# Layer 1's output stage and routing in one: tokens routed image by image, output bias added in layer 0, normalisation on ScalarE, experts read out first

## The reference, cut to what matters

```python
# x: (4, 56, 56, 256): B = 4 images of N = 3136 tokens, C = 256, float32
x = x + L0_conv_ref(gn(x), ...)            # layer 0: 7x7 neighbourhood attention, ends in out @ Wp + bp
t = to_tokens(x)
t = t + L1_attn_ref(ln(t), ...)            # layer 1: full attention, ends in out @ w_out + b_out
h = ln(t)                                  # then a mixture of 8 experts on T = 12544 tokens
probs = softmax(h @ gate_w + gate_b); idx = argmax(probs); prb = probs[idx]
pos = cumsum(one_hot(idx)) at the token - 1     # place in the expert's queue, over all images in order
kept = pos < C                             # C = ceil(1.25 * T / 8) = 1960 places per expert
y = relu(buf[e] @ w1[e] + b1[e]) @ w2[e] + b2[e]
t = t + nan_to_num(y_of_token * prb * kept)
```

## Time and profile before

| What | us |
|---|---|
| median of 3 runs | 7384.19 |
| the profiled execution | 7386.59 |
| its span, first to last instruction | 7384.8 |
| TensorE busy (93%) | 6849.5 |
| VectorE busy (73%) | 5365.9 |
| ScalarE busy (55%) | 4035.2 |
| GpSimd busy (50%) | 3717.6 |

### The profile page before, as it was taken

One profiled execution on the slowest core, in us unless ns is written; L12 is line 12 of the kernel. 1 busy time (PEld: TensorE's weight loads), 2 busy tenths in 40 slices (PEclk: granted clock), 3 DMA queues, 4 the chain that ended last, 5 costly groups with the idle time before them and its releaser, 6 DMA issues. The chain is left out here.

```text
span 7384.8 us, 151886 instructions
## 1 busy us (share of the span) xinstructions
PE 6849.5 (93%) x47456; PEld 4249.4 (58%) x47456; DVE 5365.9 (73%) x12955; ACT 4035.2 (55%) x9389; POOL 3717.6 (50%) x2394
## 2 busy tenths in 40 slices
PE   8699998989999999999999999999999998439999
PEld 5477775655555555554554554554555545338888
DVE  5599995667767767776776776777777765438888
ACT  2499992215665665665665665665665663024444
POOL 5111102215665665665665665666666665455553
PEclk9799999979999999999999999999999999769999
DMA  8534326851021021011012012012011004512221
GB/s 245 131 73 91 70 65 213 255 163 25 13 59 33 13 54 39 12 46 45 15 42 48 15 37 53 12 37 56 12 31 43 5 5 131 158 44 60 64 59 31
DMA packets 385430, 480.29 MB, mean 65 GB/s; under 512 B 64064, under 2 KB 341810, under 8 KB 380663
## 3 DMA queue, kind: packets, MB, share of 16 engines
q1 hardware_dynamic: 361991, 429.57, 22.6%
q0 software_dynamic: 22640, 40.75, 1.9%
HBM read 301.23 MB, written 188.86 MB: 66 GB/s over the span
## 5 line engine op out<-in xcount | busy, mean ns | idle before, releaser
L1418 DVE TENSOR_REDUCE a_tops<-a_ps 128x1 f32<-128x448 f32 x5600 | 3087.3, 613 | 1160.4 <-PE a_ps L1314 1138.5
L1548 POOL TENSOR_TENSOR a_added<-a_P 128x896 f32<-128x896 f32 x1344 | 2800.2, 2103 | 1776.4 <-ACT a_P L1524 1776.4
L1524 ACT ACTIVATE a_P<-a_ps 128x448 f32<-128x448 f32 (+1 forms) x5600 | 2656.5, 547 | 1806.6 <-PE a_ps L1387 1784.2
L1387 PE MATMUL a_ps<-a_qp,a_kp 98*128 98x448 f32 (+1 forms) x5600 | 2187.4, 396 | 34.0 <-ACT a_P L1524 23.1
L1314 PE MATMUL a_ps<-a_kp,a_qp 96*128 96x448 f32 x4704 | 1744.9, 381 | 0.6
L1387 PEld LDWEIGHTS a_ps<-a_qp,a_kp 98*128 98x128 f32 (+1 forms) x5600 | 1038.9, 187 | 1178.8 <-ACT a_P L1524 579.7
L1340 PE MATMUL a_ps<-a_P,a_vt 128*32 128x448 f32 (+1 forms) x11200 | 1327.6, 546 | 0.0
L1314 PEld LDWEIGHTS a_ps<-a_kp,a_qp 96*128 96x128 f32 x4704 | 879.7, 187 | 234.7 <-DVE a_tops L1418 145.7
L1356 PE MATMUL a_ps<-a_added,a_ones 128*32 128x448 f32 x5376 | 645.2, 552 | 0.0
L1340 PEld LDWEIGHTS a_ps<-a_P,a_vt 128*32 128x32 f32 (+1 forms) x11200 | 289.2, 109 | 510.9 <-issue 379.1
L682 ACT ACTIVATE n_P<-n_sm,n_mx 112x280 f32<-112x280 f32 x896 | 468.1, 522 | 96.9 <-DVE n_mx L629 96.7
(11 more groups left out here) (196 smaller groups left out, 7860.4 us busy)
## 6 DMA issues: line engine op xcount, KB each, us to landing
a_qp<-scratch_q SPq DMA_DIRECT2D x168, 224.0 KB, 3.8
a_hk<-scratch_k SPq DMA_DIRECT2D x84, 392.0 KB, 6.2
a_kp<-scratch_k SPq DMA_DIRECT2D x96, 320.0 KB, 5.0
scratch_t<-o_ts SPq DMA_DIRECT2D x56, 448.0 KB, 5.5
n_vt<-scratch_vw SPq DMA_DIRECT2D x64, 343.0 KB
e_w<-in_w SPq DMA_DIRECT2D x16, 1024.0 KB, 6.8
scratch_vw<-p_vs SPq DMA_DIRECT2D x56, 224.0 KB
...
```

The lines of the kernel that those rows point to most:

```text
L1387: pe.matmul(PS[0:rows_of(t), i_s % 3, 0:GW], kp[0:98, hh, 128 * t:128 * t + rows_of(t)], qp[0:98, hh, GW * j:GW * j + GW], start=True, sto ...
L1418: dve.tensor_reduce(tops[0:rows_of(t), slot, k:k + 1], PS[0:rows_of(t), bank, 0:GW], AX_X, ALU.max).then_inc(topped, 1)
L1524: act.activation(P[0:rows_of(t), (2 * n + pair) % (2 * RING), hh % 2, :], PS[0:rows_of(t), (4 * n + hh) % 3, 0:GW], ACT.Exp).then_inc(expe ...
L1548: pool.tensor_tensor(added2[:, a % 6, :, :], P[:, (2 * n + pair) % (2 * RING), :, :], P[:, (2 * n + 2 + pair) % (2 * RING), :, :], ALU.add ...
```

## The change

- `layer0_output`: `b_out` is loaded as well (`bob`), and GpSimd adds it to `ts` after VectorE has normalised it (`bias_of_output`), so `t0` holds it already. `store_t(k)` waits for that and stands behind `store_qkv(k-1)`.
- `layer1_output`: no bias on GpSimd. VectorE makes only the factor and the shift of each token (`factor`), and ScalarE normalises with them. The first load stands ahead of most constants.
- `route` is gone as a stage. Its work is done per image within `layer1_output`: `choose`, `rank` and `set_places` follow `logits(k)` in three successive rounds once an image's seven groups are through; `carry` takes the counts on to the next image. GpSimd clears, then scatters 28 columns per image. The copies to the result stand in SyncE's queue behind the last stores. The logits no longer pass through HBM.
- `experts`: `normalise` is cut in two (`spread_of` and `normalise`), and the first tile's `scale` stands between them.

```diff
             def store_t(k):
                 b, g = divmod(k, NG)
-                sp.wait_ge(summed, 2 * k + 2)
+                sp.wait_ge(outed, 4 * k + 4)
                 sp.dma_start(S["t0"][b, GW * g:GW * g + GW, :].rearrange("(j p) c -> p j c", p=TT), ts[:, k % RT, :, :])\
...
                 if k + 3 < G:
                     load(k + 3)
+                if k >= 1:
+                    store_qkv(k - 1)
                 if k < G:
                     store_t(k)
-                if k >= 1:
-                    store_qkv(k - 1)
...
+            def bias_of_projection(k):
                 pool.wait_ge(loaded[k % RL], 32 * (k // RL + 1))
                 for u in range(4):
                     pool.tensor_tensor(ts[:, k % RT, u, :], ts[:, k % RT, u, :], bpb[:, :], ALU.add).then_inc(biased, 1)
+
+            def bias_of_output(k):
+
+                for u in range(4):
+                    pool.wait_ge(normed, 4 * k + u + 1)
+                    pool.tensor_tensor(ts[:, k % RT, u, :], ts[:, k % RT, u, :], bob[:, :], ALU.add).then_inc(outed, 1)
+
+            bias_of_projection(0)
+            bias_of_projection(1)
+            for k in range(G):
+                bias_of_output(k)
+                if k + 2 < G:
+                    bias_of_projection(k + 2)
...
+            def copy_image(b):
+
+                for w in range(RT):
+                    sp.wait_ge(t_stored[w], 16 * len(range(w, NG * (b + 1), RT)))
+                sp.dma_start(A["out"][b].rearrange("(p r) c -> p (r c)", p=112),
+                             S["t1"][N * b:N * b + N, :].rearrange("(p r) c -> p (r c)", p=112)).then_inc(out_copied, 16)
...
+            sp.dma_start(wo[:, :, :], A["w_out"].rearrange("(c p) n -> p c n", p=128)).then_inc(consts, 16)
+            load(0)
...
-            sp.dma_start(S["logits"], lg[:, :, :]).then_inc(logits_stored, 16)
-            for k in range(RT):
-                sp.wait_ge(t_stored[k], 16 * len(range(k, G, RT)))
+                if k >= G - 3:
+                    copy_image(k - (G - 3))
+            copy_image(B - 1)
...
+            for b in range(B):
+                pool.wait_ge(placed, b + 1)
+                for j in range(NT * b, NT * (b + 1)):
+                    pool.indirect_dma_start(out=S["table"], out_offset=bass.IndirectOffsetOnAxis(ap=slotu[:, j:j + 1], axis=0),
+                                            in_=rows[:, j, :], in_offset=None, bounds_check=SLOTS - 1,
+                                            oob_is_err=False).then_inc(scattered, 16)
+            pool.wait_ge(scattered, 16 * J)
...
+            def count(b):
+                pe.wait_ge(told, b + 1)
+                if b >= 1:
+                    pe.wait_ge(placed, b)
+                cols = hot[:, :, :].rearrange("p j e -> p (j e)")
+
+                pe.matmul(PS[0:TT, RANK, 0:JE], upper[:, :], cols, start=True, stop=True).then_inc(counted, 1)
+                pe.matmul(PS[0:TT, TOTAL, 0:JE], ones[:, :], cols, start=True, stop=True).then_inc(counted, 1)
...
+            def normalise(k):
+                act.wait_ge(factored, k + 1)
+                if k >= 2:
+                    act.wait_ge(turned, CC * (k - 2) + CC)
+                for u in range(4):
+                    act.activation(xn[:, k % 2, u, :], ts[:, k % RT, u, :], ACT.Identity, bias=shift[:, k % 2, u:u + 1],
+                                   scale=rstd[:, k % 2, u:u + 1]).then_inc(normed, 1)
...
+                if k + 1 < G:
+                    normalise(k + 1)
                 take_turned(k)
                 if k + 2 < G:
                     root(act, rstd[:, k % 2, :], spread, rooted, k + 3)
+                if k % NG == 1 and k > NG:
+                    exponentials(k // NG - 1)
+            exponentials(B - 1)
 
...
-            def normalise(k):
+            def factor(k):
                 dve.wait_ge(rooted, k + 1)
                 ch.after(dve.reciprocal(rstd[:, k % 2, :], rstd[:, k % 2, :]))
-                if k >= 2:
-                    dve.wait_ge(turned, CC * (k - 2) + CC)
-                for u in range(4):
-                    dve.tensor_scalar(xn[:, k % 2, u, :], ts[:, k % RT, u, :], mv[:, k % 2, u, 0:1],
-                                      rstd[:, k % 2, u:u + 1], ALU.subtract, ALU.mult).then_inc(normed, 1)
-
-            dve.memset(zero[:, :], 0.0).then_inc(zeroed, 1)
-            dve.memset(idle[:, :], 0.0)
-            dve.wait_ge(consts, 80)
+                dve.scalar_tensor_tensor(shift[:, k % 2, :], mv[:, k % 2, :, 0], -1.0, rstd[:, k % 2, :],
+                                         ALU.mult, ALU.mult).then_inc(factored, 1)
...
+            def choose(b):
+                part = lg[:, NT * b:NT * b + NT, :]
+                if b == 0:
+                    dve.wait_ge(route_consts, 64)
...
+            def rank(b):
+                dve.wait_ge(exped, b + 1)
+                ch.after(dve.tensor_reduce(prob[:, :], e2[:, :, :], AX_X, ALU.add))
+                dve.wait_ge(counted, 2 * b + 2)
+                totals = PS[0:TT, TOTAL, 0:JE].rearrange("p (j e) -> p j e", e=EXP)
+                ch.after(dve.tensor_copy(counts[:, :, :], totals))
+                if b >= 1:
+                    ch.after(dve.tensor_tensor(counts[:, 0, :], counts[:, 0, :], carry[:, :], ALU.add))
+                for e in range(EXP):
...
+                if k >= NG:
+                    b, step = divmod(k - NG, NG)
+                    if step == 0:
+                        choose(b)
+                    if step == 1:
+                        rank(b)
+                    if step == 2:
+                        set_places(b)
+            choose(B - 1)
+            rank(B - 1)
+            set_places(B - 1)
...
-            def normalise(ch, e, p, g):
+            def spread_of(ch, e, p, g):
 
...
-                inverse_root(dve, ch, rstd[:, 4 * g:tiles[-1] + 1], mv[:, 4 * g:tiles[-1] + 1, 1], 1e-5,
-                             spread, rooted, e * SG + g + 1)
+                roots = rstd[:, 4 * g:tiles[-1] + 1]
+                dve.tensor_scalar(roots, mv[:, 4 * g:tiles[-1] + 1, 1], 1e-5, None, ALU.add).then_inc(spread, 1)
+
+            def normalise(ch, e, p, g):
+
+                tiles = range(4 * g, min(4 * g + 4, ST))
+                roots = rstd[:, 4 * g:tiles[-1] + 1]
+                dve.wait_ge(rooted, e * SG + g + 1)
+                ch.after(dve.reciprocal(roots, roots))
                 for t in tiles:
...
+                    tiles = range(4 * g, min(4 * g + 4, ST))
+                    if g < SG - 2:
+                        spread_of(ch, e, p, g + 2)
+                    elif more:
+                        spread_of(ch, e + 1, 1 - p, g + 2 - SG)
+                    scale(tiles[0])
                     if g < SG - 2:
                         normalise(ch, e, p, g + 2)
                     elif more:
                         normalise(ch, e + 1, 1 - p, g + 2 - SG)
                     if g == 0 and more:
                         tell(i + p, 1 - p)
-                    tiles = range(4 * g, min(4 * g + 4, ST))
-                    for t in tiles:
+                    for t in tiles[1:]:
                         scale(t)
-                        if t > tiles[0]:
-                            finish(t - 1)
+                        finish(t - 1)
                     finish(tiles[-1])
                 assert ch.n == CHAIN - (0 if more else 2 * LN_CHAIN), ch.n
```

246 lines of the change are left out of this document (104 added, 142 removed).

## The result

The changed kernel takes 7276.4 us (median of 4 runs, 7274.0 to 7286.7), the kernel before, beside it on the same chip, 7384.2 us (7380.0 to 7397.3). Ratio 0.9854 [0.9837, 0.9871]: 108 us less, where 151 were forecast. The direction was right, the time lies 4 us above the range.

The account below looks back on a forecast made before the run. Bounds: store landings in layer 1's output stage, GpSimd's scatters alone in routing, nearly balanced TensorE and VectorE in the experts. Terms -122 - 3 + 0 + 1 - 27 = -151 gave 7235.6, 7233 us against the runs' median; range 7200 to 7272.

Parts of the forecast that it names:

- Bound of the output stage: Layer 1's output stage: SyncE's next load waits for a store's landing, setting 6.95 us rounds; VectorE is not the limit.
- Routing, -122: Routing image by image inside layer 1's output stage lets the experts start at 6428 instead of 6549.5: 122 us less.
- Image 2 is placed at about 6341.3 + 2.2: Layer 1's output stage: image 2's places come 2.2 us after logits(23), itself taken as before at 6341.34; about 6343.5.
- small loss, from scatters sharing the DMA engines (2 us): Layer 1's output stage: lower bound of the normalisation term, a 2 us loss from scatters using the same DMA engines.
- in a round of 6.95 us this has room: Layer 1's output stage: VectorE, losing 2.1 us of normalisations a group, can fit the routing's operations into each round.
- Start of the stage, -3: Start of layer 1's output stage: earlier load and no bias work before the first sum, 3 us less, bounds 0 and 5.
- Normalisation on ScalarE, 0: Layer 1's output stage: moving normalisation off VectorE gains 0, from 2 us lost to 27 us less.
- I am wrong if the rounds shorten: Layer 1's output stage: sign against the forecast; rounds on SyncE's queue were to stay near 6.9 us.
- Layer 0, +1: Layer 0's output stage: adding the output bias on GpSimd costs 1 us more, bounds 0 and 8.
- Experts, -27: Experts: reading the first tile out before the normalisations saves 0.9 us in 30 groups, 27 us less, bounds 0 and 38.
- TensorE's pace: Rival: layer 1's output stage also falls to TensorE's pace, 27 us more gained, 7206 us; chance 0.12.
- Slow scatters: Rival: scatters beside a working VectorE take 2.0 us each, 33 us later, 7266 us; chance 0.08, plus 0.02 near 7330.

Follow-up runs that it names:

- 4: The kernel before with six buffers instead of four for yT and ts in its output stage: 7390.8 us, ratio 1.0001.
- 3: The changed kernel with all 112 scatters held back until the last image's places are known: 7362.7 us (one run).
- 12: The changed kernel with all scatters held back behind the last places, repeated on another chip: 7367.3 us, ratio 0.9949.
- 1: The changed kernel with six buffers instead of four for yT and ts in the output stage: 7251.4 us, ratio 0.9812.
- 9: The changed kernel, source unchanged, on a chip where TensorE and VectorE all but stand still while scatters run: 7360.2 us, ratio 0.9931.
- 15: The kernel before with the changed kernel's experts function and nothing else: 7382.9 us against 7409.5, ratio 0.9962.

## Why the prediction was wrong

**Bound of the output stage: half right.** The loop of the earlier trace rows was there (removing its wait changed the rounds), but "not VectorE, though that looks nearly full" was wrong: VectorE stood 0.4 us behind (4), and in the pace of `logits` 0.1.

**Routing, -122: the failed step,** measured -88 with the start of the stage. The step is "Image 2 is placed at about 6341.3 + 2.2": it takes the rounds up to `logits(23)` as they were before, and they are 39.5 us longer. Two terms of the prediction are in it.

- The "small loss, from scatters sharing the DMA engines (2 us)" is 28 to 30 us (changed kernel against 3 and 12, and 1 takes back 28), and about 100 on the other kind of chip, where the stage of 9 is 368.8 us long against 300.0. I asked what the busy engines do to the scatters, and bounded it with the earlier trace rows. I did not ask what scatters do to a loop that waits for a landing in each round, though the earlier trace rows showed that all of a longer landing becomes time. Beside the earlier trace rows, six rounds with 5 us more would have been a rival at about 7263.
- The routing's operations on VectorE, of which it says "in a round of 6.95 us this has room", cost 9 to 11 us net (3 and 12 against before). VectorE has the time: it is busy for 23.1 of the 33 us of the routing rounds in 3. But the steps, measured at 2.5, 3.2 and 3.1 us (2.0, 2.5 and 2.2 estimated), stand ahead of the factor for the next group, and TensorE waits in the end. The room was counted over the round and not at the place.

The rest of the 37 us: the places of image 2 come 4.0 us after `logits(23)`, not 2.2; `logits(0)` comes 5.0 us sooner, not 3; scatters at 1.35 us in the stage, measured 1.25; 11.5 us to the experts, measured 12. The last scatters were to stand behind a backlog of GpSimd, where in fact GpSimd waited 25.8 and 34.5 us for the places of images 1 and 2; image 3's did follow image 2's without a gap.

The Trainium skill (SBUF — State Buffer, "SBUF: two separate sides") has GpSimd's descriptor writing blocked while VectorE runs a two-port operation. No run here shows that for the table's scatters: 941 to 944 ns at the median in every trace, alone or beside VectorE, and where one side stood still it was VectorE, with TensorE slowed as well.

**Start of the stage, -3:** right, with 5 measured. From the stage's first transfer to `logits(0)` it is 24.4 us against 29.4 in the two profiles, 23.8 to 27.2 in all seventeen profiles of the new stage and 28.6 to 30.4 in three of the old. **Normalisation on ScalarE, 0:** in SyncE's closed loop, 0.25 us a quiet round (6.95 to 6.70), which by the prediction's own words ("I am wrong if the rounds shorten") is a sign against it, if a small one; what it is worth with the loop open was not tried by itself (4 and 1 differ in the change's other edits too). ScalarE's 589 ns for one (0.5 taken) cost nothing. **Layer 0, +1:** the stage is 434.2 to 436.8 us in seventeen profiles of the new code and 433.9 to 434.0 in three of the old: +2. The first transfer of `layer1_attend` stands anywhere from 1562 to 1578 us in profiles of the new code, so the other 7 us of the +9.3 are within what such code varies by.

**Experts, -27: right,** 27 to 28 by 15 and 29.7 in the two traces. The old code alone varies by 5 us between its profiles (835.4, and 830.3 in 4), so 15 is the better measure. The waits of the profile after, from 6487 to 7235:

```profile
ACT e_h L2160 <- DVE e_hTl L2237: 38.1, 28, 2.5
...
DVE e_hTl L2237 <- ACT e_hTh L2164: 21.7, 47, 0.8
...
PE e_ps L2133 <- DVE e_widest L2249: 10.0, 18, 1.0
```

The wait for the read-out went from 38.3 us to 10.0, VectorE's for ScalarE from 33.9 to 21.7, and ScalarE's for VectorE rose from 11.8 to 38.1 us, the coupling for which 0.3 us a group was set aside.

**Rivals.** TensorE's pace came only in the rounds of `logits` that neither routing nor scatters touch (5.8 to 6.1 us), and the others took more than that gave. Slow scatters fell as a mechanism. Its price, 7266 us, came nearest, by luck: slow is what stands beside them.
